# A hand-written engine order is rewritten from the causal heads to the second cross attention

## The reference

```
x = _ln(xx, ln1_g, ln1_b)
x = x + _mha(x, x, a1_..., causal=True)
x = _ln(x, ln2_g, ln2_b)
return x + _mha(x, ee, a2_..., causal=False)

_mha(x, y):
    xn, yn = _ln(x), _ln(y)
    q, k, v = heads of xn @ wq, yn @ wk, yn @ wv      # 16 heads of 32
    o = softmax(q k^T * 32 ** -0.5) (causal: times a mask) @ v
    x_out = x + o @ li1_w + li1_b
    h = gelu(_ln(x_out) @ li2_w + li2_b)
    return x_out + h @ li3_w + li3_b
```

## Time and profile before

| | |
|---|---|
| time, median of 3 | 370.5 us (369.88 to 372.94) |
| the profiled execution | 370.13 us, of which the span from first to last instruction is 368.4 us |
| mean granted TensorE clock | 0.977 |
| PE, DVE, ACT, POOL busy | 88%, 78%, 74%, 33% of the span |
| last causal products to the first scores of "a2" | 249.6 to 281.9 us |
| the 16 units | 281.9 to 334.9 us |

### The profile page before, as it was taken

How to read it: one execution, slowest core, us unless ns; L and a number is a source line. 1 busy time by engine, 2 the same in 40 slices (tenths; PEclk the granted TensorE clock), 3 DMA queues, 4 the chain that set the end, 5 groups by cost and what they waited for, 6 DMA issues and landing times. The chain is left out here.

```text
span 368.4 us, 6956 instructions
## 1 busy us (share of the span) xinstructions
PE 325.3 (88%) x2168; PEld 231.1 (63%) x2168; DVE 287.4 (78%) x738; ACT 271.0 (74%) x957; POOL 122.7 (33%) x227
## 2 busy tenths in 40 slices
PE   4989999636699788989989999989899899999997
PEld 4867988513344545655555566757566688877775
DVE  0768768787878998979898998985678887976545
ACT  2378899738445999999898999972545998892463
POOL 1316575324630332323232333331012454441110
PEclk9999999976799999999999999999999999999999
DMA  6900000000008969800992398400000000000001
GB/s 199 377 16 1 2 1 2 0 1 2 2 0 186 206 137 204 182 3 1 199 209 52 71 209 179 174 3 0 2 0 3 0 3 0 4 0 2 0 0 59
DMA packets 7052, 24.75 MB, mean 67 GB/s; under 512 B 1467, under 2 KB 1800, under 8 KB 6280
## 3 DMA queue, kind: packets, MB, share of 16 engines
q1 hardware_dynamic: 7016, 24.31, 27.4%
HBM read 7.00 MB, written 0.52 MB: 20 GB/s over the span
## 5 line engine op out<-in xcount | busy, mean ns | idle before, releaser
L1265 ACT ACTIVATE pring<-ps,nm 128x512 f32<-128x512 f32 x128 | 88.7, 721 | 6.7 <-DVE nm L1691 6.7
L1691 DVE TENSOR_REDUCE nm<-ps 128x1 f32<-128x512 f32 x128 | 80.9, 677 | 9.9 <-PE ps L725 9.7
L1144 ACT ACTIVATE arena<-ps,nmx 128x77 f32<-128x77 f32 x256 | 79.1, 346 | 11.4 <-DVE nmx L1443 11.1
L1032 POOL TENSOR_SCALAR_AFFINE_SELECT pring<-pring 128x128 f32<-128x128 f32 x128 | 37.2, 293 | 79.4 <-ACT pring L1265 79.4
L1144 ACT ACTIVATION_READ_ACCUMULATOR arena<-ps,nmx 128x1 f32 x256 | 58.2, 227 | 0.0
L725 PE MATMUL ps<-stack 128*128 128x512 f32 x128 | 53.4, 480 | 4.2 <-ACT pring L1265 3.6
L997 POOL TENSOR_TENSOR arena<-arena,rden 128x616 f32<-128x616 f32 x32 | 39.2, 1225 | 50.2 <-DVE rden L1452 50.2
L444 PE MATMUL ps<-ident,pring 128*128 128x128 f32 x320 | 47.6, 276 | 6.2 <-ACT early L1237 1.9
L444 PEld LDWEIGHTS ps<-ident,pring 128*128 128x128 f32 x320 | 36.2, 140 | 22.0 <-POOL pring L1032 11.7
L571 PEld LDWEIGHTS ps<-arena 128*128 128x128 f32 x320 | 38.9, 191 | 12.6 <-DVE arena L1459 11.2
L571 PE MATMUL ps<-arena 128*128 128x128 f32 x320 | 42.5, 280 | 3.3 <-DVE arena L1459 3.2
(11 more groups left out here) (151 smaller groups left out, 527.3 us busy)
## 6 DMA issues: line engine op xcount, KB each, us to landing
stack<-sides SPq DMA_DIRECT2D x32, 256.0 KB, 5.2
stack<-arena SPq DMA_DIRECT2D x16, 256.0 KB, 5.0
stack<-hid SPq DMA_DIRECT2D x12, 256.0 KB, 5.3
wa_sb<-in_wa SPq DMA_DIRECT2D x1, 1536.0 KB, 13.5
early<-in_w SPq DMA_DIRECT2D x2, 512.0 KB, 7.7
stack<-hid SPq DMA_DIRECT2D x8, 128.0 KB, 2.5
arena<-in_wa SPq DMA_DIRECT2D x1, 1024.0 KB, 5.1
pring<-in_wf SPq DMA_DIRECT2D x1, 768.0 KB, 10.0
```

The lines of the kernel that those rows point to most:

```text
L1032: pool.affine_select(out=blk, in_=blk, compare_op=ALU.is_gt, fill=0.0, base=0, pattern=[[1, P]], channel_multiplier=-1).then_inc(masked, 1)
L1144: ins = act.activation(Pc[:, i % PC_SLOTS, h * HS:h * HS + M], bank(where[key])[:, h % 4 * HS:h % 4 * HS + M], ACT.Exp, bias=nmx[:, i % 4, ...
L1265: release(act.activation(pring[:, n % 2, i, :], bank(f"S{i}"), ACT.Exp, bias=nm1[:, n % 8, i:i + 1], accum_out=den1[:, n % 8, i:i + 1]), ( ...
L1691: dve.tensor_reduce(nm1[:, n % 8, i:i + 1], bank(f"S{i}"), AX.X, ALU.max, negate=True).then_inc(nm1_ready, 1)
```

## The change

TensorE's list between the causal heads and the units is put in another order. The two context projections now come together, ahead of `li1(1)`; `ln_transposes("a1f", 0)` comes ahead of it too. Both feed-forward "up" stages and batch 0's "down" come ahead of all folding; the two folds run without anything in between. Of batch 1's four "down" chunks one stands ahead of the transposes of "a2", one behind, and two beside units 1 and 2, where `keep_busy` stood. The ten value transposes of batch 0 stand in unit 1. Folding uses the banks T0, T1, S2, S3 instead of T0, T1, S0, S1. Ten of its sixteen copies are ScalarE's now (four before), six are VectorE's; the values' three copies go to VectorE.

The residual, "ln2" and the "a2" norm of batch 1 are all done by VectorE beside units 2 to 6, in five pieces, and two sums of 128x512 (`xb`) move from VectorE to GpSimd, ahead of units 8 and 9. The sums of `bias_and_residual` are split by batch.

```
@@ -332,17 +333,20 @@
-                eng = "act" if n_part % 2 and (f_site, kv) in (("l0", 0), ("a2", 1)) else "dve"
+                if f_site == "l0":
+                    eng = "act" if n_part % 2 and kv == 0 else "dve"
+                else:
+                    eng = "act" if n_part < (6, 4)[kv] else "dve"
...
-                eng = "act" if b_use == 0 and (f_site == "a2" or n_part == 1) else "dve"
+                eng = "act" if (f_site, b_use, n_part) == ("l0", 0, 1) else "dve"
...
-        VO_BANKS = {"l0": ("A", "B", "T0"), "a2": ("T0", "T1", "S2")}
+        VO_BANKS = {"l0": ("A", "B", "T0"), "a2": ("T0", "T1", "A")}
...
-                banks = ("T0", "T1", "A", "B") if site == "l0" else ("T0", "T1", "S0", "S1")
+                banks = ("T0", "T1", "A", "B") if site == "l0" else ("T0", "T1", "S2", "S3")
@@ -549,8 +551,13 @@
+                    if site == "a2" and i == 1:
+                        for n in range(len(VO_GROUPS)):
+                            transpose_values("a2", 0, n, VO_BANKS["a2"][n])
                     if site == "a2" and i in (1, 2):
-                        keep_busy(5 if i == 1 else 2, "A")
+                        ffn_down_by_chunk("a1f", 1, (i + 1,))
+                    if site == "a2" and i == 7:
+                        ln_transposes("a2", 1)
@@ -582,8 +589,6 @@
-                    if site == "a2" and i == 6:
-                        ln_transposes("a2", 1)
@@ -839,30 +831,20 @@
             project_context("a2", 1)
+            project_context("a2", 0)
+            ln_transposes("a1f", 0)
             li1(1)
-            ln_transposes("a1f", 0)
-            project_context("a2", 0)
+            ffn_up("a1f", 0)
+            ffn_down_by_chunk("a1f", 0, (0, 1))
+            ln_transposes("a1f", 1)
+            ffn_down_by_chunk("a1f", 0, (2, 3))
+            ffn_up("a1f", 1)
             pe.wait_ge(loaded["wa2"], 16)
...
-            ffn_up("a1f", 0)
-            ln_transposes("a1f", 1)
-            fold("a2", 0, down_beside_fold(0))
-            ffn_up("a1f", 1)
-            fold("a2", 1, down_beside_fold(1))
-            for n in range(len(VO_GROUPS)):
-                transpose_values("a2", 0, n, VO_BANKS["a2"][n])
+            fold("a2", 0)
+            fold("a2", 1)
+            ffn_down_by_chunk("a1f", 1, (0,))
             ln_transposes("a2", 0)
-            keep_busy(3)
+            ffn_down_by_chunk("a1f", 1, (1,))
             cross("a2")
@@ -1003,7 +985,13 @@
                     if site == "a2" and j == 2:
+                        power("ln2", batches=[1])
+                    if site == "a2" and j == 4:
                         power("a2", batches=[1])
+                    if site == "a2" and j in (7, 8):
+                        pool.wait_ge(xn_ready, nth("ln2", 1))
+                        pool.tensor_tensor(xb[:, j - 7, :, :], x1[:, j - 7, :, :], row4("a2_li1_b"), ALU.add)\
+                            .then_inc(xb_ready, 1)
@@ -1278,13 +1262,14 @@
             project_context("a2", 1)
+            project_context("a2", 0)
             ln_evac("a1f", 0, ("a1_ln3_g", "a1_ln3_b"))
-            project_context("a2", 0)
             preload(ACT.Gelu)
             gelu("a1f", 0)
+            ln_evac("a1f", 1, ("a1_ln3_g", "a1_ln3_b"))
             gelu("a1f", 1)
+            fold("a2", 0)
             fold("a2", 1)
-            copy_transposed_values("a2", 0)
             ln_evac("a2", 0, ("a2_lnx_g", "a2_lnx_b"))
@@ -1478,15 +1464,17 @@
-                    if site == "a2" and i in (0, 1):
-                        ln2_bias(1, range(2 * i, 2 * i + 2))
-                    if site == "a2" and i in (2, 3):
-                        ln_stats("a2", 1, x1, range(2 * i - 4, 2 * i - 2))
-                    if site == "a2" and i in (4, 5):
-                        ln_norm("a2", 1, x1, tiles=range(2 * i - 8, 2 * i - 6))
-                    if site == "a2" and i in (6, 10):
-                        b = (6, 10).index(i)
-                        did(dve.tensor_tensor(xb[:, b, :, :], x1[:, b, :, :], row4("a2_li1_b"), ALU.add))
+                    if site == "a2" and i == 2:
+                        add_to_xb(1, "a1f")
+                    if site == "a2" and i == 3:
+                        ln_stats("ln2", 1, xo)
+                    if site == "a2" and i == 4:
+                        ln2_gain(1)
+                        ln2_bias(1)
+                    if site == "a2" and i == 5:
+                        ln_stats("a2", 1, x1)
+                    if site == "a2" and i == 6:
+                        ln_norm("a2", 1, x1)
@@ -1719,23 +1705,19 @@
-            add_to_xb(1, "a1f")
-            ln_stats("ln2", 1, xo)
-            ln2_gain(1)
             cross("a2")
```

More of the change, by code:

```diff
@@ L478, in project_context, with fold @@
                     filled(m, ("proj", site, kv, n))
-            def fold(site, kv, pair_issued=None):
+            def fold(site, kv):
                 f, src = FOLD[site], heads_kv[site][kv]
                 wx = f["wo" if kv else "wq"]
-                banks = ("T0", "T1", "A", "B") if site == "l0" else ("T0", "T1", "S0", "S1")
+                banks = ("T0", "T1", "A", "B") if site == "l0" else ("T0", "T1", "S2", "S3")
                 uses = fold_uses(site)
@@ L625, in logits @@
                 filled(m, ("logits", b))
[L627 to L638, removed]
             def ffn_down_by_chunk(site, b, chunks=range(NF), tiles=range(NT), res=None, key="out"):
@@ L1050, in _ @@
             power("ln2", "a2", batches=[0])
-            power("ln2", batches=[1])
             cross("a2")
@@ L1138, in cross @@
                         copy_transposed_values("l0", 0)
+                    if site == "a2" and i == 7:
+                        ln_evac("a2", 1, ("a2_lnx_g", "a2_lnx_b"))
                     if i < NU:
@@ L1157, in cross @@
                         round_x(0)
-                    if site == "a2" and i == 6:
-                        ln_evac("a2", 1, ("a2_lnx_g", "a2_lnx_b"))
             def gelu(site, b):
                 for k in range(NF):
-                    if site == "a1f" and k == 2 and b == 0:
-                        ln_evac("a1f", 1, ("a1_ln3_g", "a1_ln3_b"))
                     key = ("up", site, b, k)
@@ L1446, in cross @@
                         fold("l0", 1, range(0, 4))
-                    if site == "l0" and i == 2:
-                        copy_transposed_values("l0", 0, range(len(VO_GROUPS)))
+                    if site == "l0" and i == 2 or site == "a2" and i == 1:
+                        copy_transposed_values(site, 0, range(len(VO_GROUPS)))
                     if 1 <= i < NU + 1:
@@ L1530, in a2_residual, with bias_and_residual @@
                 settle()
-            def bias_and_residual(name):
-                for b in range(NB):
-                    did(dve.tensor_tensor(xb[:, b, :, :], x1[:, b, :, :], row4(name), ALU.add))
+            def bias_and_residual(b, name):
+                did(dve.tensor_tensor(xb[:, b, :, :], x1[:, b, :, :], row4(name), ALU.add))
                 settle()
-                for b in range(NB):
-                    did(dve.tensor_tensor(xb[:, b, :, :], xb[:, b, :, :], xo[:, b, :, :], ALU.add))
+                did(dve.tensor_tensor(xb[:, b, :, :], xb[:, b, :, :], xo[:, b, :, :], ALU.add))
                 settle()
@@ L1724, in _ @@
             ln_norm("a1f", 1, xo)
-            bias_and_residual("a1_li3_b")
-            fold("a2", 0)
+            bias_and_residual(1, "a1_li3_b")
             add_to_xb(0, "a1f")
@@ L1729, in _ @@
             ln2_gain(0)
-            fold("a2", 1, range(0, 4))
             ln2_bias(0)
-            fold("a2", 1, range(4, 6))
             ln_stats("a2", 0, x1)
-            fold("a2", 1, range(6, 8))
+            fold("a2", 0)
             ln_norm("a2", 0, x1)
-            add_to_xb(1, "a1f")
-            ln_stats("ln2", 1, xo)
-            ln2_gain(1)
+            fold("a2", 1)
             cross("a2")
@@ L1744, in a2_out @@
                 settle()
+            dve.wait_ge(xb_ready, 2)
             add_to_xb(1, "a2")
```

11 lines of the change are left out of this document (3 added, 8 removed).

## The result

The changed kernel took **374.08 us** (median of 13 executions, 372.99 to 395.19), the kernel before 370.41 us (median of 13). The ratio is **1.0085, interval 1.0065 to 1.0105**: slower by 0.65 to 1.05%. The forecast was 370.3 us with a range up to 373.3 and "no difference"; the time lies above the range, and 0.1 us under the 374.2 from which the prediction would have spoken of a slower kernel. In that comparison the median of four executions was 373.05 us, ratio 1.0070 [1.0055, 1.0085].

The account below looks back on a forecast made before the run. TensorE was taken as the bound inside the units. Scores 3.8 us earlier, unit 8 4.1 us later and 0.1 off for unit 0's maximum gave 370.13 + 0.2 = 370.3 us; range 366.7 to 373.3.

Parts of the forecast that it names:

- The sum: Whole kernel: -3.8 us at the first scores, +4.1 at unit 8, 0.1 off for unit 0's maximum: 370.3 us.
- the fold stretch: Eight fold pairs after `ffn_up(1)`: limited by banks, 0.85 us a pair, leaving TensorE at U + 10.3.
- U: Start of `ffn_up(1)` on TensorE, forecast at 265.2 us instead of 269.09; first scores at U + 12.9.
- walk: Step-by-step timing of the folds' banks up to the scores, and of VectorE's list beside the units up to batch 1's norm.
- own signs of being wrong: Unit 8's scores before 302, a granted clock below 1 between 270 and 305, or a fold stretch over 7 us.
- The clock rival: Idle time in units 5 to 7 and pauses between fold pairs lower TensorE's clock: 373.3 us, 376 with both; chance 0.13.
- The front: Up to the first scores: three moves cost 0.2 us, `ffn_up(1)` starts at 265.2, scores start 3.8 us earlier.
- VectorE in the units: Units 2 to 6: 7.0 us of side work against 5.3 of room; unit 8 is 4.1 us later against e.
- e: Start of the first exponential, forecast at about 280.3 us instead of 284.18; times inside the units count from it.
- The rival that the pipeline absorbs the excess: Units: only 1.7 us or less of VectorE's excess is lost, 366.3 to 368.3, about 367.8 us; chance 0.22.

Follow-up runs that it names:

- e8: The changed kernel plus one unread 512-column bf16 matmul behind every second pair of folds, four in all: 370.96 us, ratio to the kernel before 1.0023.
- e0: The changed kernel run once more without any edit, profiled in an undisturbed execution: median 373.05 us, ratio to the kernel before 1.0070.
- e1: The changed kernel plus one unread 512-column bf16 matmul behind each of the eight pairs of folds: 371.93 us, ratio to the kernel before 1.0050.
- e6: The changed kernel with batch 1's ln2 gain and bias done for one tile of four (result not the reference's): 371.66 us, ratio to before 1.0013.
- e5: e4 with folds in S0 and S1, batch 1's sum, ln2 statistics and gain ahead of the units, the rest in halves beside units 0 to 5: 367.59 us.
- e4: The changed kernel with folds in four groups of two pairs, batch 1's down chunks between and behind them, copies alternating ScalarE and VectorE: 370.96 us.
- e11: The changed kernel with each fold matmul of the second cross attention issued twice, 64 instead of 32: 372.92 us, ratio to the kernel before 1.0069.

## Why the prediction was wrong

**The step that failed is the price and the chance of the clock in the folds.** The sum took the fold stretch as "limited by its banks, not by its matmuls" and counted U + 12.9 with TensorE at 2.4 GHz throughout. Its walk was right as long as the clock was: counted from the measured U it puts the start of the sixth pair at 273.5, and the row is at 273.64. Then the clock fell. Against the walk the folds ended 1.29 us late (U + 11.59 for 10.3), the down chunk took 1.87 for 0.89, and from the transposes to the scores it was 2.13 for 1.70: together 2.7 us, the 15.59 in place of 12.9. e8 puts the clock back with four unread matmuls, and returns 2.4 us of this at the scores and 1.7 to 2.1 us of the time. Two of the prediction's own signs of being wrong had come: a clock below 1 between 270 and 305, and a fold stretch over 7 us (8.1, from 269.20 to 277.33).

**The clock rival named the mechanism and put it in the wrong place.** It spoke of the 1.8 and 2.0 us of idle time in units 5 to 7 first and of "pauses between fold pairs" in half a sentence, and said that only a fall of both would go over 1%. The units did stand idle for 1.54 and 1.65 us, and kept their clock; the folds, which TensorE's record shows nearly full, lost it (e0 again, the units first):

```profile
299.00:305.00 6.00, 3.50 (x24) 2.90 (x25) 5.84 (x21) 5.09 (x32) 3.43 (x3) 1.00 0.00 0
273.00:274.00 1.00, 0.77 (x9) 0.56 (x8) 1.00 (x5) 0.59 (x2) 0.20 (x1) 0.76 0.00 0
```

The evidence that was weighed, 2.80 busy of 5 us before a fall and 3.09 of 5 without one, compares busy times, and that is what misled. The row of folds reads as nearly full, though it runs at less than half the pace of folds that wait for nothing. The kernel before gave a hint that was not used: it never issued more than two pairs of folds before the next down matmuls (0.82 us at 272.62), and the change put all eight in a row. The price of one fall, 3 us, was somewhat high against e8's 1.7 to 2.4. That rival's 373.3, the edge of the range, lies between the two medians: e0, with this fall, took 373.05, and the rest of the way to 374.08 is the 1.0 us between the two comparisons that no profile explains. The rival deserved more than 0.13, because a stretch which was made of one kind of thin work for 8 us was new.

**The front is right.** U was forecast at 265.2; in the profiles it lies at 265.11 to 265.95, but for the one with the fall in `li1(1)` (e1). The wait behind `li1(1)` is gone, and 0.44 and 0.96 us have come ahead of the second projection and of `li1(1)`; the net cost at `ffn_up(0)` was forecast as 0.2 and is 0.47. U is 0.47 late by another sum: 0.34 from the execution, 0.3 from this cost, and some 0.15 less from `ffn_up(0)` to U than forecast (7.44 for 7.6). VectorE is not late: "ln2" and the "a2" statistics of batch 0 end at 272.1, forecast 271.5.

**VectorE in the units is right**, nearly step by step. VectorE's timeline of e0:

```profile
295.20 1.73 DVE L1369 SCALAR_TENSOR_TENSOR x<-sides,mv,rows_sb 128x128 f32<-128x128 f32 x4
296.96 1.14 DVE L1376 SCALAR_TENSOR_TENSOR x<-x,rstd,rows_sb 128x128 f32<-128x128 f32 x4
298.13 0.80 DVE L1428 TENSOR_REDUCE nmx<-ps 128x8 f32<-128x616 f32 x1
...
302.68 1.64 DVE L1333 TENSOR_SCALAR xn<-x,mv,rstd 128x128 f32<-128x128 f32 x4
```

The maximum of unit 5 starts at e + 14.59 (14.6 in the walk), unit 8 at e + 23.49 (23.8). The rival that the pipeline absorbs the excess falls: e6 took 1.57 us out and got 1.56 back, and e5 took the pieces ahead, with the transposes of batch 1 back in iteration 6, and got back all 3.8. The gain took 1.73 beside GpSimd's scaling and 1.13 alone, so 0.60 more, as forecast; the norm took 1.64 and 1.11 alone (the prediction's sum has 1.15), so 0.53 for the forecast 0.4. GpSimd's scaling beside the gain kept its length (GpSimd's timeline, with an `xb` sum below):

```profile
294.76 1.23 POOL L979 TENSOR_TENSOR arena<-arena,rden 128x616 f32<-128x616 f32 x1
...
310.51 1.27 POOL L993 TENSOR_TENSOR sides<-x,rows_sb 128x512 f32<-128x512 f32 x1
```

The Trainium skill, "SBUF — State Buffer", section "Who interferes with whom", has VectorE and GpSimd exclude each other for such instructions; the trace agrees in that the gain, which started 0.79 us before the scaling ended, grew by three quarters of that. The statistics beside unit 5, which read one operand, overlapped a scaling by 0.64 us and took 0.86, against 0.87 alone. The `xb` sums on GpSimd took 1.27 and 1.28, forecast by the scaling's 1.23, and TensorE did not wait for them.

**The sum**, with the clock held, was right to 0.7 us: -3.3 at the first exponential and +3.8 behind it in e4 and e8, where -3.8 and +4.1 had been forecast. Both terms were too large by 0.3 to 0.6, and the two misses cancel in part; that is luck.

## What to carry to other kernels

When work is taken out from between small matmuls, ask what is left for TensorE in the microseconds after it, and price a fall of the clock there: here one fall cost 1.5 to 2.4 us, and no other term of the sum was off by more than 0.5. Don't judge it by the busy share of the record alone; put useful work that has to be done anyway between thin matmuls (e4), and use unread matmuls only if there is none, as few as hold the clock (e8's four cost less than e1's eight). And an earlier start of a pipeline is worth what its slowest helper lets through: the early start (3.3 us in e4) came out in the time only when VectorE's side work went back ahead of the units (e5, 2.6 us at the first exponential and 3.0 in the time).

## What the runs showed of the hardware

- The clock fell to 1.2 GHz while TensorE was recorded busy 3.51 of 4 us, with no pause over 0.24 us. It stayed at 2.4 GHz with 3.50 busy of 6 us and idle stretches of 1.54 and 1.65 us among matmuls of 128 rows. The recorded busy share doesn't tell these two apart. The Trainium skill, "TensorE: Matmul & The Clock Gate", section "What's actually happening", says that half rate is the default and activity releases it. e8 and e11 agree in kind, as more work in the same place was enough.
- One 0.39-us bf16 matmul of 512 columns for every two pairs of folds, or each fold matmul twice, held the clock. By what measure the chip tells these rows from e0's, the runs don't say.
